# A graph layer with LayerNorm on one Trainium2 core: product chunks spread over about twenty places, u in pieces, LayerNorm's two sums by ScalarE's accumulator, the last products in three pieces

## What is computed

```python
Ws = 0.5 * (W + jnp.swapaxes(W, -1, -2))
A = jax.nn.sigmoid(U @ U.T)
K = Ws * A[None, :, :]
deg = jnp.maximum(K.sum(axis=-1), EPS)
d = jax.lax.rsqrt(deg)
K = K * d[:, :, None] * d[:, None, :]
y = w_scale * jnp.einsum('bnm,bmc->bnc', K, x)
out = _layernorm(x + y, axis=-1)      # over the 64 values of a row
```

## Time and profile before

| | |
|---|---|
| median of 3 runs | 531.81 us (526.47, 531.81, 533.03) |
| profiled execution, its own time | 527.15 us |
| its span | 525.3 us |
| busy TensorE / VectorE / ScalarE / GpSimd | 433.0 / 421.1 / 210.2 / 118.4 us |
| mean granted TensorE clock | 0.971 |
| DMA | 143.08 MB, 272 GB/s over the span |

### The profile page before, as it was taken

One profiled execution on the slowest core, in us unless ns is written; L12 is line 12 of the kernel. 1 busy time (PEld: TensorE's weight loads), 2 busy tenths in 40 slices (PEclk: granted clock), 3 DMA queues, 4 the chain that ended last, 5 costly groups with the idle time before them and its releaser, 6 DMA issues.

```text
span 525.3 us, 14322 instructions
## 1 busy us (share of the span) xinstructions
PE 433.0 (82%) x5256; PEld 235.8 (45%) x5256; DVE 421.1 (80%) x1137; ACT 210.2 (40%) x654; POOL 118.4 (23%) x132
## 2 busy tenths in 40 slices
PE   4887789787888789798888789788898889787791
PEld 4555434454445443554345434454354544554230
DVE  5788746999779978999779968899779977999333
ACT  3697421454224531453234531453234541454200
POOL 0000000004410254004410244004410244004611
PEclk9799899999999999999999989999999999999797
DMA  8996569984999689994999669995999679990011
GB/s 281 387 356 240 182 230 365 353 264 168 351 381 285 202 298 357 338 337 167 329 393 307 222 239 353 340 340 190 325 384 309 224 278 371 339 326 0 1 41 40
DMA packets 102857, 143.08 MB, mean 272 GB/s; under 512 B 37296, under 2 KB 37296, under 8 KB 102832
## 3 DMA queue, kind: packets, MB, share of 16 engines
q1 hardware_dynamic: 88240, 139.08, 75.1%
q10 hardware_dynamic: 14592, 3.67, 3.3%
HBM read 138.54 MB, written 4.19 MB: 272 GB/s over the span
## 4 chain that ended last, share of the span: by engine, by line
PE 60%; ACT 11%; issue 10%; DMA 9%; DVE 7%; SPq 1%; POOLq 0%; POOL 0%; DVEq 0%; ACTq 0%
PE yp L387 35%; PE kt L345 13%; ACT k L489 9%; DMA out_dram<-h 7%; PE tw L345 7%; PE yp L469 3%; DVE k L572 2%; DVE k L583 2%; PE yp L416 2%; DMA k<-in_adj_dram 2%; ACT gate L480 1%; SPq L203 1%; DMA h<-in_L_gnn_U_dram 1%; DVE h L619 1%; PE tw L452 1%
## 5 line engine op out<-in xcount | busy, mean ns | idle before, releaser
L489 ACT ACTIVATE k<-kt 128x512 f32<-128x512 f32 (+3 forms) x288 | 149.6, 524 | 266.3 <-PE kt L345 266.2
L572 DVE TENSOR_TENSOR k<-tw,k 128x512 f32<-128x512 f32 (+2 forms) x320 | 193.3, 604 | 66.2 <-PE tw L345 56.2
L387 PE MATMUL yp<-k,z 128*64 128x512 f32 x928 | 219.5, 610 | 0.6 <-issue 0.4
L583 DVE CUSTOM_DVE_ANT_0 k<-k,gate 128x512 f32<-128x512 f32 (+2 forms) x320 | 202.4, 633 | 0.3 <-ACT gate L480 0.3
L345 PE MATMUL kt<-ident,k 64*128 64x64 f32 x1920 | 93.5, 229 | 70.7 <-ACT k L489 61.5
L345 PEld LDWEIGHTS kt<-ident,k 64*128 64x128 f32 x1920 | 76.2, 140 | 99.7 <-issue 99.4
L387 PEld LDWEIGHTS yp<-k,z 128*64 128x64 f32 x928 | 61.3, 139 | 100.3 <-issue 95.8
L345 PEld LDWEIGHTS tw<-ident,k 64*128 64x128 f32 x2176 | 82.7, 140 | 49.9 <-issue 49.8
L345 PE MATMUL tw<-ident,k 64*128 64x64 f32 x2176 | 100.2, 228 | 1.7 <-DMA k<-in_adj_dram 0.9
L277 POOL TENSOR_TENSOR d<-deg,minus_half 128x4 f32<-128x4 f32 x32 | 34.3, 1071 | 254.4 <-DVE deg L593 254.2
L489 ACT ACTIVATION_READ_ACCUMULATOR k<-kt 128x1 f32 x288 | 57.2, 199 | 0.0
(11 more groups left out here) (60 smaller groups left out, 130.4 us busy)
## 6 DMA issues: line engine op xcount, KB each, us to landing
k<-in_adj_dram SPq DMA_DIRECT2D x128, 1024.0 KB, 7.2
xt<-in_x_dram ACTq DMA_DIRECT2D x7, 512.0 KB, 5.9
out_dram<-h SPq DMA_DIRECT2D x7, 512.0 KB, 8.9
xt<-in_x_dram SPq DMA_DIRECT2D x1, 512.0 KB, 13.9
out_dram<-k SPq DMA_DIRECT2D x2, 256.0 KB, 2.6
h<-in_L_gnn_U_dram SPq DMA_DIRECT2D x1, 128.0 KB, 3.9
ws<-in_L_gnn_w_scale_dram ACTq DMA_DIRECT2D x1, 0.5 KB, 3.3
```

The lines of the kernel that those rows point to most:

```text
L387: t = pe.matmul(yp[at:at + C, m // 2, :], z[:, n * G + c, :], K[(n, m)][:, c, :], start=(q == first_unit[m] and c == 0), stop=(q == last_u ...
L489: nc.scalar.activation(K[(j, i)][:, r, c0:UW].rearrange("p (c h e) -> p c h e", h=2, e=H), whole_rows(kt[:, 0:2, :], r % 2, (UW - c0) // P ...
L572: nc.vector.tensor_tensor(row, whole_rows(tw[:, tw_bank[g] // 2 * 2:tw_bank[g] // 2 * 2 + 2, :], g % 2, w // P), row, ALU.add).then_inc(su ...
L583: nc.vector.tensor_tensor_reduce(row, row, A[:, A_AT[g]:A_AT[g] + w], 1.0, 0.0, ALU.mult, ALU.add, deg_parts[:, i * G + r, j:j + 1]).then_ ...
```

## The change

It does five things.

1. `PRODUCT_ROWS` spreads the 32 chunks: at most two at a row, four in a pair of rows, and at least one in 18 of the 20 pairs of rows; `UPPER_LAG` goes from 2 to 3, which puts uppers at odd rows, behind the chunks of both rows of a pair. Three pairs of units instead of two are done within the graph's own round. Degrees, z, copies, scaling, adding, centering and dividing move by some rows (the last divide from row 89 to row 100).
2. VectorE's two reductions over 128 x 1024 and ScalarE's square over 128 x 1024 go. In their place ScalarE runs 16 copies and 16 squares of 128 x 64, each with its accumulator, two at a row (`sum_rows`, `sum_squares`), and the mean is made in two halves.
3. u is loaded so that a partition holds four successive rows (256 bytes instead of 64 in a piece), and is split, transposed and copied in four pieces; pieces 1 to 3 are transposed and copied within rows 0 to 2 of the first round. Fourteen transposes of the identity run ahead, and a Sigmoid of one column loads ScalarE's table early.
4. The tail's products: bank 0 whole, then bank 1 in two halves of 256 columns, the second summed in a bank of its own (`kt`) and added by `join_last_y`. LayerNorm of the last graph runs in these three pieces of 8, 4 and 4 groups, its last parts interleaved.
5. The last pieces are stored in halves, the last half by ScalarE's queue.

```diff
-UPPER_LAG = 2
-PRODUCT_ROWS = [29, 29, 31, 31, 37, 37, 37, 37, 41, 41, 41, 41, 45, 45, 45, 45, 45, 45, 48, 48, 48, 48, 48, 48, 53, 53, 57, 57, 62, 62, 62, 64]
-DEG_ROWS = [25, 34, 40, 43]
-Z_ROWS = [26, 37, 43, 45]
-KEEP_ROW = 61
-SCALE_ROW = 51
-COPY_ROWS = [58, 65]
-Y_ROWS = [64, 67]
-Y_SCALE_ROWS = [64, 67]
-ADD_ROWS = [71, 72, 73, 74]
-MEAN_ROW = 76
-CENTER_ROWS = [76, 77, 78, 79]
-SQUARE_ROW = 80
-VAR_ROW = 82
-DIVIDE_ROWS = [86, 87, 88, 89]
+UPPER_LAG = 3
+PRODUCT_ROWS = [30, 30, 33, 33, 34, 35, 37, 37, 38, 38, 39, 39, 41, 41, 43, 44, 45, 45, 47, 48, 48, 49, 51, 52, 55, 56, 57, 58, 61, 62, 64, 64]
+DEG_ROWS = [25, 33, 40, 44]
+Z_ROWS = [26, 33, 42, 45]
+KEEP_ROW = 56
+SCALE_ROW = 60
+COPY_ROWS = [56, 64]
+Y_ROWS = [62, 66]
+Y_SCALE_ROWS = [66, 70]
+ADD_ROWS = [66, 68, 72, 77]
+SUM_ROW = 76
+MEAN_ROWS = [79, 83]
+CENTER_ROWS = [79, 82, 83, 84]
+SQUARE_ROW = 83
+VAR_ROW = 91
+DIVIDE_ROWS = [92, 95, 97, 100]
+SUMS_PER_ROW = 2
...
+UT_ROWS = [0, 0, 1, 2]
+WARM = 14
...
+LAST_PAIRS = [[n for n in PAIRS[OWN:] if n[0][1] // 2 == k] for k in range(2)]
+PIECES = [(0, 0, G), (1, 0, G // 2), (1, G // 2, G)]
+PIECE_Y_AFTER = 5
...
-            def square(b):
-                act.wait_ge(centered, LN_PARTS * (b + 1))
-                nc.scalar.activation(y_sb[:, :, :].rearrange("p k w -> p (k w)"),
-                                     h[:, :, :].rearrange("p n c -> p (n c)"), ACT.Square).then_inc(squared, 1)
+            def sum_rows(b, n):
+
+                if n % G == 0:
+                    act.wait_ge(h_ready, LN_PARTS * b + (n // G + 1))
+                if n == 0:
+                    act.wait_ge(var_ready, b)
+                nc.scalar.activation(y_sb[:, n // 8, (n % 8) * C:(n % 8 + 1) * C], h[:, n, :], ACT.Copy,
+                                     accum_out=mean[:, n:n + 1]).then_inc(h_summed, 1)
+
+            def sum_squares(b, n):
+
+                if n % G == 0:
+                    act.wait_ge(centered, LN_PARTS * b + (n // G + 1))
+                if n == 0:
+                    act.wait_ge(rstd_ready, b)
+                nc.scalar.activation(y_sb[:, n // 8, (n % 8) * C:(n % 8 + 1) * C], h[:, n, :], ACT.Square,
+                                     accum_out=var[:, n:n + 1]).then_inc(sq_summed, 1)
...
-            def row_mean(b):
-                dve.wait_ge(h_ready, LN_PARTS * (b + 1))
-                nc.vector.tensor_reduce(mean[:, :], h[:, :, :], AX_X, ALU.add).then_inc(h_summed, 1)
-                dve.wait_ge(h_summed, b + 1)
-                nc.vector.tensor_scalar(mean[:, :], mean[:, :], -1.0 / C, None, ALU.mult).then_inc(mean_ready, 1)
+            def row_mean(b, k):
+                dve.wait_ge(h_summed, NC * b + 8 * (k + 1))
+                nc.vector.tensor_scalar(mean[:, 8 * k:8 * k + 8], mean[:, 8 * k:8 * k + 8], -1.0 / C, None,
+                                        ALU.mult).then_inc(mean_ready, 1)
...
+            for piece, (k, c0, c1) in enumerate(PIECES):
+                columns = slice(c0 * P, c1 * P)
+                chunks = [(pair, c) for pair in LAST_PAIRS[k] for c in range(G)]
+                for at, (pair, c) in enumerate(chunks):
+                    if piece and at == PIECE_Y_AFTER:
+                        transpose_last_y(piece - 1)
...
+                        t = pe.matmul(y, z[:, n * G + c, :], K[(n, m)][:, c, columns],
+                                      start=(c0 > 0 and at == 0), stop=(at == len(chunks) - 1))
+                t.then_inc(last_done, 1)
+            transpose_last_y(len(PIECES) - 1)
```

More of the change, by code:

```diff
@@ L437, in steps @@
                     if lags == 1:
+                        for k in range(1, G):
+                            if UT_ROWS[k] == row:
+                                transpose_u(k)
                         for g in range(gates_before(row), gates_before(row + 1)):
@@ L528, in beside @@
                         copy_y(b, k, first)
[L529 to L530 removed]
+                for n in range(16):
+                    if due(row, lag, SUM_ROW + n // SUMS_PER_ROW):
+                        sum_rows(b, n)
+                for n in range(16):
+                    if due(row, lag, SQUARE_ROW + n // SUMS_PER_ROW):
+                        sum_squares(b, n)
             def steps(b, lags):
@@ L534, in steps @@
                     if lags == 1:
+                        for k in range(1, G):
+                            if UT_ROWS[k] == row:
+                                copy_u(k)
                         for g in range(gates_before(row), gates_before(row + 1)):
@@ L639, in beside @@
                         scale_y(b, k)
-                if due(row, lag, MEAN_ROW):
-                    row_mean(b)
+                for k in range(2):
+                    if due(row, lag, MEAN_ROWS[k]):
+                        row_mean(b, k)
                 if due(row, lag, VAR_ROW):
```

279 lines of the change are left out of this document (174 added, 105 removed).

## The result

The changed kernel takes 498.52 us (median of 4 runs, 495.75 to 499.21) beside 531.58 us of the kernel before: ratio 0.938, 95% interval 0.931 to 0.946. The predicted 488 us was 10.5 us too low; the range of 474 to 509 holds the result. Executions more than 1.5% above the fastest of their kernel are left out of every ratio, but not out of the medians. Its profiled execution took 499.21 us, its span is 497.4 us.

The account below looks back on a forecast made before the run. The prediction took alternating waits of TensorE and VectorE, caused by clumped chunks, as the bound. Second round at 71.5 + 7 rounds x 54.3 + tail 32.5 = 484 us of span; 488 us predicted as time, range 474 to 509.

Parts of the forecast that it names:

- TensorE's sum, 48 us a round: TensorE's work in a round of the new order, from 0.55 us per 16 transposes and 0.88 us a chunk: 48 us.
- It just fits: Loads from row 37 to unit (3,0) at row 56: 26.3 us against 25 us of rows and VectorE's lag of 2.
- The round, 54.3 us: Each round after the first: 56 us by pairs of rows, less 5, plus 3; between 52 and 57 us.
- The start: First addition at 9.5 to 10 us instead of 13.30, second round beginning at about 71.5 us instead of 73.1.
- The 3 us put down for new waits: Allowance in each round for VectorE's new waits at the degrees and z, with load waits left inside it: 3 us.
- the 5 that the rings win back: Buffering's gain in each round against the sum of the larger engine per pair of rows: 56 - 5 = 51 us.
- ScalarE: size right, use wrong: ScalarE's 32 new instructions at 0.25 us, 8 us a round, hidden beside the uppers because TensorE needs longer.
- The tail: From the last round's start to the end: 32.5 us instead of 37.8, with 9 instead of 11.4 behind the last matmul.
- the "no change" case: Rival, chance 0.09: late releases after row 48 let loads decide; rounds stay at 58 to 59 us, time 520 to 525.
- the rival of VectorE held by new waits: Rival, chance 0.20: uncovered degree-row stalls and a late (3,0) cost 3 us more a round; time 509 us.
- ScalarE's serial short instructions: Rival, chance 0.05: ScalarE's short sums run serially; at 0.8 us each, rounds of 62 us and a time of 540.
- The clock falls: Rival, chance 0.06: TensorE's clock falls once a round, 1.7 us each, 12 us over seven rounds; time 500 us.

Follow-up runs that it names:

- e1: The changed kernel with the product rows of before, up to six chunks at a row: 538.75 us, ratio 1.010 to the kernel before.
- e8: The kernel before with only the row tables of the change; sums on VectorE, old start and tail: 498.04 us, ratio 0.928.
- e10: The changed kernel with four of each graph's 32 chunks left out: 497.37 us in the profiled execution, 505.55 to 508.29 in three others; no ratio given.
- e12: The changed kernel with half-unit loads from the second graph on and four chunks a graph left out: 469.69 us, ratio 0.885 to the kernel before.
- e13: The changed kernel with the first pairs' chunks some rows earlier and LayerNorm's sums back on VectorE: 491.73 us, ratio 0.927 to the kernel before.
- e2: The changed kernel with LayerNorm's sums back on VectorE: 494.84 us, ratio 0.928 to the kernel before.
- e11: The changed kernel with the first pairs' chunks some rows earlier, so units are released earlier: 491.92 us, ratio 0.926 to the kernel before.
- e4: The changed kernel with the tail's last products in two whole-bank pieces instead of three: 498.50 us, ratio 0.932 to the kernel before.

## Why the prediction was right, and where it was not

- **What bounds the kernel: right.** The alternating waits of clumped chunks were the loss. With the chunks clumped again (e1) the gain is gone; with the row tables alone (e8) it is whole. TensorE's wait before uppers came to 13.0 us (below 15 was named), VectorE's for tw to 19.2 (below 30), TensorE's share to 90% (above 88).
- **TensorE's sum, 48 us a round: too small.** The windows show 51.4 to 53.2. The mis-sized term is the chunk: I took 5.30 / 6 = 0.88 us from a block of six. The change makes blocks of one to four, and each block has a cost of its own. In the kernel after:

```profile
250.97 2.80 PE L441 MATMUL yp<-k,z 128*64 128x512 f32 x12
253.69 0.28 PE L399 MATMUL kt<-ident,k 64*128 64x64 f32 x2
...
254.34 1.08 PE L441 MATMUL yp<-k,z 128*64 128x512 f32 x4
255.35 0.71 PE L399 MATMUL kt<-ident,k 64*128 64x64 f32 x16
```

  Three chunks take 2.72 us from start to start and one 1.01, so a chunk is 0.855 and a block adds 0.155. Eighteen blocks a round make 32 x 0.855 + 18 x 0.155 = 30.2 us; the sum had 32 x 0.88 = 28.2, so 2 us too few. The rest of the shortfall is older than the change: the same prices gave 47 us for the order before, where the earlier trace rows have 50.2. What the finer blocks really added is eight of them, 1.2 us, and TensorE went from 50.2 us to 51.4 and 52.2 us in two rounds with the clock at 1.00. By e10 and e12 only a part of such a sum reaches the round, so this is a part of the missing 1.6 us at most.
- **VectorE's sum, 49 us: right** (47.9 to 48.7).
- **"It just fits": the step that failed.** I had the load of (3,0) land as its row comes, left VectorE's wait for loads at 9.5 us and took loads to exclude only rounds below 52 us. In the kernel after, row 16 of one round, where (3,0) is due, and row 12 of the next, where (2,0) is:

```profile
264.89 0.69 DVE L691 TENSOR_TENSOR k<-tw,k 128x512 f32<-128x512 f32 x1 [1.18 <-DMA k<-in_adj_dram]
...
315.00 0.69 DVE L691 TENSOR_TENSOR k<-tw,k 128x512 f32<-128x512 f32 x1 [2.62 <-DMA k<-in_adj_dram]
```

  (3,0) is late by 1.0 to 1.2 us in three of the six whole rounds. Not priced in the sum were two units ahead of it in the queue: (2,0) is late by 0.9 to 2.6 us in four rounds, (1,0), at row 4, by 0.5 to 1.7 us in four. It is 15.6 us in all instead of 9.5. From the issue of the pair released at row 37 to the landing of (3,0) the round with the row above has 28.4 us (236.34 to 264.78), where 26.3 were taken. And 46 us for a round's 17.8 MB counted only bandwidth at its best: the windows have 0.93 to 0.95 of the DMA engines' time in 55.3 to 56.3 us, some 52 us. With the loads off the chain (e13, where no whole round has a fall of the clock either) a round is 54.7 us, so loads may account for up to 1.2 of the 1.6 us that were missing; that they account for all of it isn't shown.
- **The round, 54.3 us: 55.9 measured**, 7 x 1.6 = 11 us. The start adds 2.8 and the tail takes 0.4 off, so the span is 13.4 us above the 484 of the sum. That the time is only 10.5 us off is luck: 4 us were put on top of the span, and the median lies 1.1 above it. The 3 us put down for new waits and the 5 that the rings win back were chosen as a pair against a sum that had neither the blocks' cost nor the loads in it.
- **ScalarE: size right, use wrong.** An instruction of 64 columns is 0.246 us long, and with its accumulator read the next follows 0.24 us later where they stand together (237.08 to 237.32 above); 0.25 was taken. By the fixed part and the overlap in the Trainium skill, page "ScalarE: Activation LUTs", section "What ACT_TABLE_LOAD costs", the estimate was 0.15 us from one to the next; with the accumulator in use the measured 0.24 decides. ScalarE is busy 30.1 us a round instead of 23.4, and this wasn't hidden as the prediction had it: VectorE waits 2.2 us a round for the sums, as much as the two reductions would have cost it, and the time is the same with them back on VectorE (e2, and e13 beside e11).
- **The waits around the degrees were named at the right places** (degrees behind ScalarE 11.3 us, z behind GpSimd 11.8 us; 23.1 / 8 graphs = 2.9 us, beside the 3 us put down for new waits; the kernel before had 4.3 us of them in all). Not foreseen was the mean's wait for ScalarE, 15.5 us.
- **The start: the first addition was right in kind (7.91 us, predicted 9.5 to 10), its worth not.** The second round was to begin at 71.5 and began at 74.31. What the sum left out is TensorE's clock in the first round, 24 us of it at 0.50 in this execution beside 14 us before; in the nine kernels with 7 to 14 us of it the second round began at 67.6 to 72.3, around the forecast.
- **The tail: right in size** (32.1 us, predicted 32.5; from the last chunk's end at about 489.3 to the end 8 us, predicted 9). Of the 6.1 us gained behind the last row's degrees e4 gives the pieces 1.4, and the row tables alone 4.9 (e8), with fewer chunks left over.
- **The rivals.** Loads, at 0.09 the "no change" case, are waited for 2.1 us a round (8.6 us in the four from 186.72 us on), and the round is 1.6 us above the forecast and not the 4 to 5 that the case needed; the rival of VectorE held by new waits has its waits (15.5, 11.8, 11.3 us), and half of its 3 us a round on top. ScalarE's serial short instructions didn't come: its busy time is 30 of 56 us. The clock falls for 3.4 us in three of the six whole rounds (PEclk 0.97 instead of 1.00); these took 55.1, 56.3 and 57.7 us, the other three 55.3, 55.9 and 56.5. How finely the chunks are cut doesn't decide it: e1, with blocks of up to six, has a fall in every round, e13, with blocks of one to four, in none of its six whole ones.
